# Attention output kept as a rounded half and its remainder in DRAM, so that the first FFN layer loads both and splits nothing

## The reference, cut to what matters

```python
x = x + _L0_xattn_ref(_layernorm(x), ctx_2048, ...)   # 16 query heads of 128, 4 groups; softmax; out @ wo
x = x + _L0_ffn_ref(_layernorm(x), w1, w2)            # both linears quantised
x = x + _L1_xattn_ref(_layernorm(x), ...)             # scores against 256 context rows, top 54 kept
x = x + _L1_ffn_ref(_layernorm(x), w_gate, w_up, w_down, ln_weight)

# _L0_ffn_ref: activations rounded to 127 levels of the row's maximum,
# weights to -1, 0, 1 times gamma = mean(|w|)
h = bitlinear(x, w1)            # 512 -> 2048
h = jnp.square(jax.nn.relu(h))
return bitlinear(h, w2)         # 2048 -> 512
```

## Time and profile before

| what | value |
|---|---|
| median of 3 runs | 1679.57 us (1678.8 to 1679.74) |
| profiled execution | 1677.97 us |
| its span, first to last instruction | 1676.7 us |
| mean granted TensorE clock | 0.969 of full speed |
| PE busy | 1531.6 us, 91% of the span, 8842 instructions |
| DVE busy | 1243.3 us, 74% |
| ACT busy | 923.8 us, 55% |
| POOL busy | 777.6 us, 46% |
| DMA | 123.17 MB, mean 73 GB/s |

### The profile page before, as it was taken

One profiled execution on the slowest core, in us unless ns is written; L12 is line 12 of the kernel. 1 busy time (PEld: TensorE's weight loads), 2 busy tenths in 40 slices (PEclk: granted clock), 3 DMA queues, 4 the chain that ended last, 5 costly groups with the idle time before them and its releaser, 6 DMA issues.

```text
span 1676.7 us, 26671 instructions
## 1 busy us (share of the span) xinstructions
PE 1531.6 (91%) x8842; PEld 1194.6 (71%) x8842; DVE 1243.3 (74%) x2967; ACT 923.8 (55%) x2468; POOL 777.6 (46%) x896
## 2 busy tenths in 40 slices
PE   5899999999999999999987789999997789999987
PEld 4778888888888888888875556666665566666653
DVE  4677676676766767667767867888888878888774
ACT  3565666666666656666664254334434356666655
POOL 2454555555555555555654222222224355555443
PEclk8999999999999999999997899999999799999999
DMA  6010010100101001002243354444445101111000
GB/s 258 7 33 32 26 45 20 32 32 26 43 22 32 32 23 42 26 32 85 105 158 133 105 183 151 151 151 150 151 123 205 50 16 49 51 51 39 26 14 26
DMA packets 50825, 123.17 MB, mean 73 GB/s; under 512 B 5888, under 2 KB 6016, under 8 KB 49280
## 3 DMA queue, kind: packets, MB, share of 16 engines
q1 hardware_dynamic: 50688, 121.46, 21.3%
HBM read 96.27 MB, written 25.17 MB: 72 GB/s over the span
## 4 chain that ended last, share of the span: by engine, by line
PE 58%; DVE 28%; issue 5%; ACT 4%; POOL 4%; DMA 1%; SPq 0%; DVEq 0%; ACTq 0%; POOLq 0%
PE bank L281 11%; PE bank L311 9%; PE bank L364 8%; PE quad L351 4%; PE bank L1129 4%; PE bank L1181 3%; DVE r L1359 3%; PE quad L339 2%; PE quad L341 2%; PE quad L340 2%; DVE bh L2036 2%; DVE wk L1992 2%; PE quad L1156 2%; PE quad L1691 2%; PE bank L1599 2%
## 5 line engine op out<-in xcount | busy, mean ns | idle before, releaser
L529 ACT ACTIVATE Pt<-Pt,small 128x384 f32<-128x384 f32 (+1 forms) x256 | 172.8, 682 | 119.0 <-DVE small L750 118.9
L364 PE MATMUL bank<-PT,vv 128*128 128x512 f32 x672 | 200.2, 406 | 12.0 <-DVE PT L735 11.9
L311 PE MATMUL bank<-wq,xT 128*128 128x512 f32 x768 | 207.0, 405 | 4.2 <-DVE wq L645 3.3
L946 POOL TENSOR_SCALAR Pt<-Pt,small 128x384 f32<-128x384 f32 (+1 forms) x256 | 162.8, 650 | 98.5 <-DVE small L758 98.5
L1129 PE MATMUL bank<-wq,ot 128*128 128x512 f32 x768 | 199.1, 414 | 5.3 <-DVE xr L1292 4.4
L750 DVE CUSTOM_DVE_ANT_0 Pt<-quad,mask,small 128x384 f32<-128x384 f32 (+1 forms) x256 | 171.0, 678 | 24.9 <-PE quad L341 23.5
L735 DVE TENSOR_TENSOR PT<-quad,PT 128x512 fp32r<-128x512 f32 x224 | 153.9, 687 | 48.0 <-ACT PT L521 47.6
L1129 PEld LDWEIGHTS bank<-wq,ot 128*128 128x128 f32 x768 | 149.7, 198 | 40.3 <-issue 7.6
L1413 POOL TENSOR_TENSOR ot<-oraw,ot 128x512 fp32r<-128x512 f32 x64 | 85.4, 1345 | 165.4 <-ACT ot L1226 165.4
L311 PEld LDWEIGHTS bank<-wq,xT 128*128 128x128 f32 x768 | 137.9, 190 | 30.8 <-DVE wq L645 4.6
L934 POOL TENSOR_TENSOR t<-t 128x512 f32<-128x512 f32 x64 | 84.2, 1315 | 151.2 <-DVE t L716 151.2
(11 more groups left out here) (270 smaller groups left out, 3566.5 us busy)
## 6 DMA issues: line engine op xcount, KB each, us to landing
ot_scratch<-OT SPq DMA_DIRECT2D x64, 256.0 KB, 2.0
oraw<-ot_scratch SPq DMA_DIRECT2D x64, 256.0 KB, 2.8
wkv_f<-in_w SPq DMA_DIRECT2D x12, 512.0 KB, 5.2
wkc_f<-in_w SPq DMA_DIRECT2D x12, 512.0 KB, 6.4
wkv_f<-in_wg SPq DMA_DIRECT2D x11, 512.0 KB, 4.7
wkv_f<-in_wd SPq DMA_DIRECT2D x11, 512.0 KB, 5.7
wkv_f<-in_wu SPq DMA_DIRECT2D x10, 512.0 KB, 4.3
stg<-in_ctxT SPq DMA_DIRECT2D x16, 256.0 KB, 2.7
```

The source lines that it names most:

```text
L311: ins = pe.matmul(bQ[:], xT[p][:, k, qt * 128:qt * 128 + 128], wq[j][:, g, k, :], start=(part == 0 and k == 0), stop=(part == 2 and k == 3))
L364: ins = pe.matmul(bO[:], vv[x][:, bg % 2, kt, :], PT[y][:, k % 2, :], start=(kt == 0 and n == 0), stop=(kt == tiles_in(i) - 1 and n == 2))
L529: act.activation(p, p, ACT.Exp, bias=nm[:, i % 2, h:h + 1], scale=-1.0, accum_out=sm[:, i % 2, h:h + 1]).then_inc(f["s_exp"], 1)
L946: pool.tensor_scalar(p, p, ri[:, i % 2, h:h + 1], 1.0, ALU.mult, ALU.mult).then_inc(f["p_n"], 1)
```

## The change

The attention stores each output as two halves. ScalarE's copy now writes the high half of `OT` (type fp32r), and a new VectorE instruction, `dve_o_lo(i - 2)`, subtracts it from `bO` to give the low half. In an even step it stands behind the second score eviction, ahead of `dve_q_ve`; in an odd step behind `dve_q_ve`, ahead of `dve_p_lo(i - 1, 0)`. The next `pe_pv` into `bO` and the store (512 KB, twice as much) wait for it. The FFN loads 512 KB chunks straight into the four slots of `ot`, each freed by `y_mm` of the chunk four earlier; `act_ot`, `pool_ot` and `oraw` are gone.

In the first tile the order is changed: on TensorE `pe_y(0,3)` comes ahead of the sum of w2; on VectorE the ternary chunk 5 of w1 moves into step 64, `dve_norm(0)` comes first in the layer, then chunks 6 and 7 of w1, and then gamma and the chunks of w2; `pe_up(0)` waits for all of w1. On SyncE the four chunks of tile 0 are loaded together in step 62 and the next ones are issued further ahead. The unused descriptor scratch is halved to make room, and `cl` is placed elsewhere.

```diff
-    OT = sb(st, "OT", [128, 512], F32)
+    OT = sb(st, "OT", [128, 2, 512], F32R)
...
             sp.wait_ge(f["k_rope"], NU // 2)
+            sp.wait_ge(f["q_mm"], NBLK)
+            sp.wait_ge(f["kv_mm"], NU)
             sp.wait_ge(f["ot0"], 16 * 56)
-            for c in range(3):
+            for c in range(4):
                 ffn["sp_ot"](c)
             sp_w2_sums(1)
-        if i == 64:
-            ffn["sp_ot"](3)
         if i >= 63:
             ffn["sp_w2"](i - 63)
+        if i == 64:
+            sp.wait_ge(f["qt_mm"], NBLK)
+            sp.wait_ge(f["kt_mm"], NU)
+            ffn["sp_x"](0)
+            for c in range(4, 7):
+                ffn["sp_ot"](c)
...
-            sp.wait_ge(f["o_cp"], p + 1)
-            sp.dma_start(ot_dram[2 * (p // 8) + p % 2, p // 2 % 4], OT[:]).then_inc(f["ot0"], 16)
+            sp.wait_ge(f["o_lo"], p + 1)
+            sp.dma_start(ot_dram[2 * (p // 8) + p % 2, p // 2 % 4], OT[:].bitcast(F32)).then_inc(f["ot0"], 16)
...
-            after(pe, f["o_cp"], i)
+            after(pe, f["o_lo"], i)
...
-        act.copy(OT[:], bO[:]).then_inc(f["o_cp"], 1)
+        act.copy(OT[:, 0, :], bO[:]).then_inc(f["o_hi"], 1)
...
+    def dve_o_lo(i):
+        if i < 0:
+            return
+        dve.wait_ge(f["o_hi"], i + 1)
+        dve.tensor_tensor(OT[:, 1, :], bO[:], OT[:, 0, :].bitcast(F32), ALU.subtract).then_inc(f["o_lo"], 1)
...
     def sp_ot(c):
         if c < 4 * NT:
-            after(sp, f["ot_lo"], c - 2)
-            sp.dma_start(oraw[:, c % 3, :], ot_dram[c // 4, c % 4]).then_inc(f[f"g_ot{c % 3}"], 16)
+            after(sp, f["y_mm"], c - 3)
+            if c == 4 * (NT - 2):
+                sp.wait_ge(f["ot0"], 16 * NBLK)
+            sp.dma_start(ot[:, c % 4, :, :], ot_dram[c // 4, c % 4]).then_inc(f[f"g_ot{c % 4}"], 16)
...
         c = 4 * n + g
-        pe.wait_ge(f["ot_lo"], c + 1)
+        pe.wait_ge(f[f"g_ot{c % 4}"], 16 * (c // 4 + 1))
...
     def pe_up(n):
         pe.wait_ge(f["xq"], n + 1)
+        if n == 0:
+            pe.wait_ge(f["w_ter"], 8)
...
     def pe_program():
+        pe_y(0, 3)
         pe_w2_sum()
-        pe_y(0, 3)
...
-    def act_ot(c):
-        if c >= 4 * NT:
-            return
-        act.wait_ge(f[f"g_ot{c % 3}"], 16 * (c // 3 + 1))
-        after(act, f["y_mm"], c - 3)
...
-        act.copy(ot[:, c % 4, 0, :], oraw[:, c % 3, :]).then_inc(f["ot_hi"], 1)
...
         v.did(dve.memset(eps, 1e-5))
+        dve_norm(0)
+        mem["dve_ternary"](0, 6)
+        mem["dve_ternary"](0, 7)
         dve.wait_ge(f["w_sum"], 2)
         mem["dve_gamma"](1, bM[:, 0:8])
         for q in range(3):
             dve_w2(q)
-        dve_norm(0)
...
-    def pool_ot(c):
-        if c >= 4 * NT:
-            return
-        pool.wait_ge(f["ot_hi"], c + 1)
-        pool.tensor_tensor(ot[:, c % 4, 1, :], oraw[:, c % 3, :], ot[:, c % 4, 0, :].bitcast(F32),
-                           ALU.subtract).then_inc(f["ot_lo"], 1)
...
-        ot = sb(once, "ot", [128, 4, 2, 512], F32R)
-        oraw = sb(once, "oraw", [128, 3, 512], F32)
+        ot = sb(once, "ot", [128, 4, 2, 512], F32)
+        sb(once, "ot_gap", [128, 3, 512], F32)
...
-        ot_dram = nc.dram_tensor("ot_scratch", (NT, 4, 128, 512), F32, kind="Internal").ap()
+        ot_dram = nc.dram_tensor("ot_scratch", (NT, 4, 128, 2, 512), F32, kind="Internal").ap()
```

More of the change, by code:

```diff
@@ L554, in act_last @@
                 act_wo(p)
-            for c in {(62, 0): (0, 1), (62, 1): (2,), (64, 1): (3,)}.get((i, half), ()):
-                ffn["act_ot"](c)
-            for q in {(60, 1): (0, 1), (61, 1): (2, 3), (63, 1): (4,), (64, 1): (5, 6, 7)}.get((i, half), ()):
+            for q in {(60, 1): (0, 1), (61, 1): (2, 3), (63, 1): (4,), (64, 0): (5, 6), (64, 1): (7,)}.get((i, half), ()):
                 act_w2_abs(q)
@@ L775, in dve_last @@
             dve_w1_gamma()
-        for q in {(62, 0): (0,), (62, 1): (1, 2), (63, 0): (3,), (63, 1): (4,), (64, 1): (5, 6, 7)}.get((i, half), ()):
+        for q in {(62, 0): (0,), (62, 1): (1, 2), (63, 0): (3,), (63, 1): (4,)}.get((i, half), ()):
             if q == 0:
@@ L786, in dve_even @@
         dve_ev(i, 1)
+        dve_o_lo(i - 2)
         if i in (0, 2, 4):
@@ L793, in dve_even @@
         dve_p_lo(i - 1, 1)
+        if i == NBLK:
+            mem["dve_ternary"](0, 5)
         dve_ri(i, 0)
@@ L897, in dve_program @@
         dve_even(NBLK)
+        dve_o_lo(NBLK - 1)
     def pool_c_lo(c):
@@ L1086, in sp_program @@
         sp_w2(2)
-        sp.wait_ge(f["ot0"], 16 * NBLK)
-        sp_x(0)
-        sp_ot(4)
+        sp_ot(7)
+        sp_x(1)
         sp_w2(3)
[L1091 to L1095, removed]
+        sp_ot(8)
         for n in range(NT):
-            sp_ot(4 * n + 11)
+            if n != 1:
+                sp_ot(4 * n + 9)
             if n == NT - 2:
@@ L1103, in sp_program @@
                 l1["sp_weights"]()
-            sp_ot(4 * n + 12)
+            if n != 1:
+                sp_ot(4 * n + 10)
             sp_x(n + 2)
@@ L1107, in sp_program @@
                 sp_w(range(3, 6))
-            sp_ot(4 * n + 13)
-            sp_ot(4 * n + 14)
+            sp_ot(4 * n + 11)
+            sp_ot(4 * n + 12)
+            if n == 0:
+                sp_ot(13)
+                sp_ot(14)
             if n < NT - 2:
@@ L1422, in pool_program @@
     def pool_program():
-        for c in range(3, 6):
-            pool_ot(c)
-        pool_rs(0)
-        for c in range(6, 8):
-            pool_ot(c)
-        for n in range(NT):
-            pool_ot(4 * n + 8)
-            pool_ot(4 * n + 9)
-            pool_rs(n + 1)
-            pool_ot(4 * n + 10)
-            pool_ot(4 * n + 11)
+        for n in range(NT):
+            pool_rs(n)
         l1["pool_xn"](0)
@@ L2300, in place @@
             mem[k] = [w[:, c * 2048:c * 2048 + 2048] for c in range(4)]
-        mem["ffn0_memory"] = (ot, oraw, xn, sb(once, "xr", [128, 3, 512], F32), sb(once, "xh", [128, 512], F16),
+        mem["ffn0_memory"] = (ot, xn, sb(once, "xr", [128, 3, 512], F32), sb(once, "xh", [128, 512], F16),
                               sb(once, "xq", [128, 512], BF16), sb(once, "r", [128, 2048], F32),
-                              sb(once, "hh", [128, 2048], F16), sb(once, "cl", [128, 2, 32], F32))
+                              sb(once, "hh", [128, 2048], F16), mem["cl"])
 def block_kernel(nc, a, out):
```

32 lines of the change are left out of this document (7 added, 25 removed).

## The result

The changed kernel takes 1650.01 us (median of 4 runs, 1649.19 to 1650.54) where the kernel before, beside it, takes 1679.65 (4 runs, 1678.8 to 1681.93). The ratio is 0.9821 with a 95% interval of 0.9804 to 0.9838: 29.6 us, or 1.8%, faster. The forecast was 1653 us, with a range of 1646 to 1666. The profiled execution took 1649.19 us, with a span of 1647.9 against 1676.7.

The account below looks back on a forecast made before the run. TensorE bounds the attention; in the FFN tiles TensorE and VectorE wait for each other, VectorE late through GpSimd splits. Terms -23 - 2 - 4 + 3 = -26 us from 1679.57 gave 1653.6, forecast as 1653, range 1646 to 1666.

Parts of the forecast that it names:

- The FFN tiles: Tiles 1 to 13: without GpSimd splits stretching VectorE, TensorE sets 19.55 us a tile; 258.15 becomes 235.5, -23 us.
- The clock: FFN tiles: granted clock of 0.98 taken to recover once waits before the transposes go, about 5 of the 23 us.
- The loads hold: FFN tiles: doubled 512 KB loads take 5.2 us with 14 us available, traffic about 220 GB/s; costed at nothing.
- Tile 0 to 1: First FFN tile, VectorE the path: lines 1300 and 1359 get shorter by 0.96 and 1.06, -2.0 us.
- The opening: Step 62 to tile 0: copies and splits gone, a chunk moved, against normalisation waits and low halves; -4 us, bounds 0 and -8.
- The attention: 64 low halves fit VectorE idle time except in step 5 of seven batches, 0.4 each; +3 us, bounds 0 and +10.
- Second layer: Stores and the second layer: nothing changes behind tile 14, the store of `OT` is off every path; 0.
- the low half costs in every step: Rival, attention: the low half delays TensorE's values product, up to 0.61 us in 64 steps, +39, 1690 us; chance 0.08.
- the splits don't stretch VectorE: Rival: GpSimd splits are not what stretches VectorE, so the FFN tiles stay; about 1676 us; chance 0.03.
- VectorE or a load last: Rival, FFN tiles: VectorE or a load still ends last, half of the 23 us stays; 1665 us; chance 0.12.
- a longer opening: Rival, opening: doubled loads ahead of w2's second half and SyncE's new waits, +6 instead of -4; 1663 us; chance 0.07.

Follow-up runs that it names:

- e8: The changed kernel plus four unused GpSimd subtractions in each of FFN tiles 1 to 12, the first timed to meet line 1353; 1669.23 us.
- e9: The changed kernel plus only one unused GpSimd subtraction in each of tiles 1 to 12, the one beside line 1353; 1658.32 us.
- e3: The changed kernel with four ScalarE copies of 128x512 put back at the old places in each of tiles 1 to 12; 1648.04 us.
- e12: The changed kernel plus timed GpSimd subtractions (both inputs from one place) and four ScalarE copies in each of tiles 1 to 12; 1663.21 us.
- e2: The changed kernel plus GpSimd fills of 128x1024 that only write, at four places in each of tiles 1 to 12; 1648.26 us.
- e11: The changed kernel itself, unaltered, run again as reference beside the other runs; 1647.78 us.
- e4: The changed kernel with the old order of the first tile on VectorE and TensorE, loads and low halves kept; 1648.53 us.
- e5: The changed kernel without the 64 VectorE low-half subtractions, the low half filled with zeros once; 1644.57 us.
- e7: The changed kernel with ternary chunks 5, 6 and 7 of w1 each one place earlier and step 62's low half ahead of the first score eviction; 1651.22 us.
- e6: The kernel before with only the descriptor scratch set to 8192 bytes; 1681.24 us.
- e1: The changed kernel plus four unused GpSimd subtractions in each of tiles 1 to 12, the first ending before line 1353 began; 1652.6 us.

## Why the prediction was right, point by point

*The FFN tiles, -23: right in size and in cause.* Measured -21.9. Line 1359, now 1353, is at 1.28 in all 32 executions, TensorE's floor of 19.55 us a tile measured 19.62, the wait in tile 8 is 0.46 for the 0.3 forecast. e8 shows that the reading of SBUF by GpSimd beside VectorE was the cause of 17.6 us, e9 that line 1353 alone gives 0.93 in each tile, and e3 and e12 that ScalarE's copies gave nothing. The other 4.2 us between e8 and the kernel before can be read tile by tile. One more tile of the kernel before is at the lower clock, 1.4. Tile 12 to 13 is 0.9 longer, because e8 has no subtraction beside line 1353 of tile 13. In the other eleven tiles together, the clock aside, it is 1.9: 0.10 to 0.16 without a pair and 0.19 to 0.26 with one in most of them, as line 1359 took 2.34 for 2.23 and line 1334 2.32 for 2.19. So no part is left over for the old loads, which were not put back.

The Trainium skill, page "SBUF — State Buffer", section "Who interferes with whom", was named for the cause, with the stretch a little too long by its rule, and it is so again. By "whoever issues first gets the shared pair for the whole instruction", line 1353 of e8 would end 1.28 us behind GpSimd's end at 1030.95, at 1032.23; it ended at 1032.03. The same section says that a GpSimd instruction that only writes does not contend with the second input of a VectorE instruction, and that a `tensor_scalar` contends with GpSimd while it runs in a two-port mode. Line 1328 (1.28 in e2) agrees with the first. Line 1294 (1.15 in e2, 1.50 in e8), a `tensor_scalar` with one input in SBUF, fits the second, but no run shows the mode in which it ran.

*The clock, 5 us of these: the size about right, the reason only in part.* The granted clock rose from 0.98 to 1.00 and TensorE's busy time fell from 239.73 to 233.77. Three tiles of the kernel before (1 to 2, 4 to 5, 12 to 13) stood at 0.92, with 1.4 us more of TensorE busy in each, 4.3 of the 6.0. The changed kernel had none in its first profile, and one in e11. Tile 1 to 2 before and in e11:

```profile
979.21:1001.44 22.23, 21.07 (x100) 14.17 (x101) 14.37 (x27) 11.36 (x19) 5.81 (x5) 0.92 0.61 204
```

```profile
969.91:990.78 20.87, 20.76 (x100) 14.16 (x102) 12.39 (x27) 8.30 (x15) 0.55 (x1) 0.92 0.68 237
```

The prediction took the fall as gone with the waits before the transposes. For tile 1 to 2 that does not hold. There the fall begins behind the waits of 1.37 and 1.22 us before the transposes of tile 1 (968.08 and 969.91 in e11), which the change leaves: e4, e5, e7 and e11 show the fall, and the first profile has the same two waits and none. Later tiles fell only in kernels with the waits (two before, four in e6, one in e8) and in none of the eight profiles without GpSimd's reads; but e1, e9 and e12 have the waits and no fall there. That the waits bring the later falls is likely and not shown.

*The loads hold.* Right: in the tiles TensorE waited for no load in 576 projection matmuls, the loads took 3.8 us in the median where 5.2 were reckoned with, and 216 GB/s were moved for the 220 forecast.

*Tile 0 to 1, -2*: measured -3.7 (29.87 to 26.18, the latter in e11 too). The two stretches came off nearly as forecast: the down product begins 0.7 us earlier behind the transposes, and line 1353 takes 1.05 less. The other 1.9 is the down product, which the sum held constant: its matmuls took 5.14 us at a granted clock of 0.67 before and 3.23 at 1.00 after (3.24 in e11). Why the clock is full there now is open.

*The opening, -4*: the term that was mis-sized most. From `pe_kv(63)` to the transposes of tile 0 it was 88.61 us (949.34 - 860.73) and is 80.98, -7.6 (-5.9 in e11). Two steps of its sum fail. First, the gain of 2 us for a chunk in idle time and the loss of 5 for the early normalisation were one thing counted at two places, and e4 shows them at nothing together. VectorE's work is the path there; whether TensorE waits for x or for h is all that the order decides. Second, the low halves cost at least 1.95 and not 1.3, because in steps 62 to 64 no `pe_kv` stands between the scores and the values product to cover them: the wait of 2.03 at 878.41 is for `OT` itself. The rest of the sum, -7.8 for splits and copies gone, then stands against -7.6 - 1.95 = -9.6 measured, or -7.9 by e11. Of it, the second instructions of the four ternary chunks gave 4.5 for the 3.6 counted: 2.17, 2.18 and, in chunks 1 and 3, 3.29 and 2.17 us became 1.28, 1.28, 1.28 and 1.51.

*The attention, +3*: the step that failed. The stall in step 5 of each batch was forecast at 0.4 us. The new wait is where the prediction put it, 0.21 us at the values product at 543.27. But before, TensorE waited 0.48 us at a later product of the same step (546.96), and that wait is gone: from the `pe_kv` of this step to the next it is 15.02 us before and 15.01 after. The prediction costed the new wait and did not ask what wait behind it would take it up. The x loads were issued at 543.01, 2.2 us later in the step as forecast, and VectorE did not wait for them. e5, with no low half at all, is not faster to `pe_kv(63)`. It was right that VectorE's idle time covers the low halves; the sum wrongly charged each batch.

*Second layer, 0*: right within the 2.3 us by which this stretch varies.

The sum of -26 was 3.6 us short of the 29.6 between the medians. By the terms, the attention was 3 us too dear, the opening 2 to 3.6 too poor and tile 0 1.7 too poor; the tiles were 1 to 2.4 too rich, and the rest is the spread between executions. That the spans differ by 28.8, and so by only 2.8 from the forecast, is in part luck: the two stretches that the change does not set came out 4.4 us longer in this profile.

*The rivals.* That the low half costs in every step is refuted by e5, that the splits don't stretch VectorE by e1 and e8; VectorE or a load last, and a longer opening, did not come.

## What to carry to other kernels

If one instruction has two lengths in a trace, lay the other engine's timeline beside it: the difference, times the executions on the way to the engine that bounds, gives the price of the meeting, and whether it lies on that way decides more than its length does (0.95 us cost 0.93 a tile at line 1353; the same stretch of line 1294 alone cost 0.02). Work moved into an idle gap has to be costed beside what the other engine does in that gap: 1.28 us became 3.26. A new wait costs only what no old wait behind it takes up. A wait for a new result is cheap as long as some independent work of the waiting engine stands ahead of it; look for the places, at the end of a loop above all, where this work is missing.

## What the runs showed of the hardware

A GpSimd fill that reads nothing lengthened a one-input VectorE instruction on SBUF from 0.55 to 1.15 us, and left a two-input one at 1.28; GpSimd's subtraction lengthened both, by 0.95. Line 735, with one input in PSUM and one in SBUF, took 0.68 us at 539.85 beside a GpSimd instruction of 128x512 on two SBUF inputs that began at 539.86, and no execution of it took more than 0.69. A GpSimd subtraction of 128x512 took 1.29 us with two input places and 1.04 with one, and the stretch of VectorE shrank with it, from 0.95 to 0.68. The first weight loads landed up to 2 us apart from one execution to the next.
